# GNN kernel on one core: the adjacency build without PSUM clears, every product issued twice

## The reference, cut to what matters

```python
def _L0_gnn_ref(h, edge_src, edge_dst):
    ...
    for i in range(3):
        msg = tmp[edge_src]
        agg = jax.ops.segment_sum(msg, edge_dst, num_segments=n)
        tmp = tmp + agg / deg[:, None]
        res = res + tmp / (1.0 + i)
    return res
...
h = jnp.maximum(_layernorm(x), 0.0);  x = x + _L0_gnn_ref(h, src, dst)
h = jnp.maximum(_layernorm(x), 0.0);  x = x + _L1_gnn_ref(...)   # scatter means, MLP
h = jnp.maximum(_layernorm(x), 0.0);  x = x + _L2_gnn_ref(...)   # attention over edges
h = jnp.maximum(_layernorm(x), 0.0);  x = x + _L3_gnn_ref(...)   # equivariant convolution
```

## Time and profile before

| | us |
|---|---|
| median of 3 runs | 2495.79 |
| lowest and highest run | 2492.46 and 2499.66 |
| span of the profiled execution | 2205.5 |
| build, first to last matmul of line 1769 | 67.1 to 338.0 |
| PE, DVE, ACT busy, share of the span | 74%, 81%, 50% |

### The profile page before, as it was taken

The page is one execution under the profiler, slowest core; times in us unless marked ns, Lnnn a source line. Parts: engine busy times, 40 slices in busy tenths (PEclk is TensorE's granted clock), DMA queues, the critical chain, the costliest instruction groups (busy, mean ns, idle before and its releaser), DMA issues.

```text
span 2205.5 us, 36859 instructions
## 1 busy us (share of the span) xinstructions
PE 1640.1 (74%) x8603; PEld 1281.5 (58%) x8603; DVE 1788.0 (81%) x5309; ACT 1113.4 (50%) x2935; POOL 865.1 (39%) x861
## 2 busy tenths in 40 slices
PE   3656667998998998735678777776657788888876
PEld 2322226887887886524567676676635555555555
DVE  8898887998998995886777877878577877777776
ACT  1766666876886983200234334243544444444443
POOL 2000000000000000077777777773037777777772
PEclk8886668999999999856788888798758878777777
DMA  6355558664765764156666566563112222222221
GB/s 215 108 150 149 155 157 270 245 247 155 268 242 194 267 249 180 34 162 163 168 163 177 163 158 186 161 184 103 48 52 54 55 56 55 55 55 54 56 55 46
DMA packets 192504, 314.88 MB, mean 143 GB/s; under 512 B 25905, under 2 KB 139448, under 8 KB 182450
## 3 DMA queue, kind: packets, MB, share of 16 engines
q1 hardware_dynamic: 163344, 248.12, 34.7%
q0 software_dynamic: 27712, 63.56, 11.3%
q10 hardware_dynamic: 1250, 0.86, 0.2%
HBM read 232.38 MB, written 80.07 MB: 142 GB/s over the span
## 4 chain that ended last, share of the span: by engine, by line
POOL 24%; DVE 13%; PE 13%; issue 12%; DMA 2%; ACT 1%; SPq 1%; DVEq 0%; POOLq 0%; ACTq 0%
POOL G L704 13%; POOL G L689 7%; POOL SCR L689 5%; PE PS L1930 2%; PE PS L2037 2%; DVE HOT_R L1187 2%; PE PS L1931 2%; PE PS L1906 2%; PE PS L1821 1%; DVE GROUPED_R L1202 1%; DVE GROUPED_R L1196 1%; DMA G<-table,src_idx 1%; ACT HB L726 1%; SPq L608 1%; DVE SCR L1362 1%
## 5 line engine op out<-in xcount | busy, mean ns | idle before, releaser
L689 POOL DMA_INDIRECT G<-table,src_idx x252 | 271.2, 1076 | 969.6 <-DMA table<-RX 889.3
L704 POOL DMA_INDIRECT G<-table,gather_idx x415 | 407.4, 982 | 249.4 <-issue 123.7
L2037 PE MATMUL PS<-SCR,OH 128*128 128x256 f32 x830 | 283.0, 506 | 107.7 <-DVE SCR L1660 104.6
L2037 PEld LDWEIGHTS PS<-SCR,OH 128*128 128x128 f32 x830 | 201.6, 252 | 160.6 <-DVE SCR L1660 121.4
L1821 PE MATMUL PS<-ALL_R 128*128 128x256 f32 (+3 forms) x2025 | 267.3, 289 | 21.7 <-DVE ALL_R L1250 9.1
L1906 PE MATMUL PS<-RX,OH 128*128 x830 | 178.4, 370 | 137.3 <-DVE SCR L1362 85.8
L1821 PEld LDWEIGHTS PS<-ALL_R 128*128 128x128 f32 (+1 forms) x2025 | 252.3, 191 | 24.6 <-DVE ALL_R L1250 9.5
L1906 PEld LDWEIGHTS PS<-RX,OH 128*128 128x128 f32 x830 | 148.3, 245 | 168.9 <-issue 163.7
L1930 PE MATMUL PS<-AT 128*128 128x128 f32 x830 | 203.9, 332 | 20.0 <-issue 11.5
L1781 PE MATMUL PS<-HOT_R,GROUPED_R 128*119 128x448 f32 x830 | 194.0, 381 | 24.7 <-DVE G L1208 23.3
L1769 PE MATMUL PS<-AT,G 128*128 128x400 bf16 x474 | 142.8, 450 | 81.1 <-ACT PS L819 51.1
(11 more groups left out here) (395 smaller groups left out, 3425.2 us busy)
## 6 DMA issues: line engine op xcount, KB each, us to landing
ALL_R<-adjacency SPq DMA_DIRECT2D x72, 1600.0 KB, 6.9
adjacency<-ALL_R SPq DMA_DIRECT2D x26, 1600.0 KB, 7.4
AT<-gathered_rows SPq DMA_DIRECT2D x103, 256.0 KB, 3.8
gathered_rows<-G SPq DMA_DIRECT2D x63, 256.0 KB, 2.3
AT<-dst_in_block SPq DMA_DIRECT2D x103, 128.0 KB, 4.0
gathered_rows<-SCR SPq DMA_DIRECT2D x40, 256.0 KB, 2.2
G<-table,gather_idx POOLq DMA_INDIRECT x415, 2.6
G<-table,src_idx POOLq DMA_INDIRECT x252
```

Of the source, the lines that this page charges most:

```text
L689: pool.indirect_dma_start(score_rows(i)[:, q], None, tables[0], bass.IndirectOffsetOnAxis(ap=src_idx[:, v:v + 1], axis=0)).then_inc(s(f"sc ...
L704: pool.indirect_dma_start(G[:, p, q, :], None, tables[i], bass.IndirectOffsetOnAxis(ap=gather_idx[:, p, q:q + 1], axis=0)).then_inc(s(f"{n ...
L2037: ins = pe.matmul(PS[:, q, 0:MSG], OH[:, p, q, :], view(SCR, M_AT + (p * VB + q) * MSG, [[1, MSG]]), start=True, stop=True)
```

## The change

ACT no longer clears PSUM. Instead each visit's product is issued twice by PE, with the same operands: once overwriting (`start=True`) and once adding (`start=False`). For a visit that opens a slot, the overwriting product goes to the slot's bank and the adding one to the next slot's bank; for a visit that continues a slot, the adding product goes to the slot's bank and the overwriting one to the next slot's. What lands in the next slot's bank is overwritten when that slot is opened. A batch can now touch one bank more, so it holds 6 visits in place of 7 (`AV`), and there are 99 batches (`AB`) in place of 85. Two tables of bank offsets are loaded for each batch, 7 words and 6 words, in place of one of 8. PE waits on `pair_copied` (with an offset of 4 that ACT adds at the start) in place of `banks_zeroed`. The tables are made by DVE (four small instructions in place of three) and POOL (`place_banks`, five instructions on one partition, put between two attribute gathers); PE and ACT wait once for them.

```diff
-AV = 7
+AV = 6
-        bank_words = begins[0:1, 2 * NT + 602:2 * NT + 602 + AB * BANK_W].bitcast(I32)
+        BANK_W = 8
+        begin_words = begins[0:1, WORDS_AT:WORDS_AT + AB * BANK_W].bitcast(I32)
+        add_words = means[0:1].rearrange("p a b -> p (a b)")[:, 0:AB * BANK_W].bitcast(I32)
...
-                sp.wait_ge(s("pair_copied"), min(PER_BLK * (b + 1) + OVER, SLOTS) // 2)
+                sp.wait_ge(s("pair_copied"), OPEN + min(PER_BLK * (b + 1) + OVER, SLOTS) // 2)
...
+            def place_banks():
+
+                pool.wait_ge(s("words_made"), 1)
+                at = lambda offset, n: view(EI, offset, [[1, n]], 1).bitcast(I32)
+                pool.memset(at(STEP_AT, 1), 1)
+                pool.tensor_tensor(at(STEP_AT + 1, AB * AV - 1), at(SLOT_AT + 1, AB * AV - 1), at(SLOT_AT, AB * AV - 1), ALU.subtract)
+                pool.tensor_tensor(span, begin_at, add_at, ALU.subtract).then_inc(s("banks_paired"), 1)
+                pool.wait_ge(s("banks_paired"), 1)
+                pool.tensor_tensor(span, span, opens, ALU.mult).then_inc(s("banks_paired"), 1)
+                pool.wait_ge(s("banks_paired"), 2)
+                pool.tensor_tensor(add_at, add_at, span, ALU.add)
+                pool.tensor_tensor(begin_at, begin_at, span, ALU.subtract).then_inc(s("banks_paired"), 1)
...
+                if g == 1:
+                    place_banks()
...
+            act.wait_ge(s("banks_paired"), 3)
             copy_fills(KINDS_AT, LAST_ATTRS)
...
-            zeros2 = view(zeros_b, 0, [[0, 2], [1, KEYS]])
-            for j in range(BANKS // 2):
-                act.copy(banks(j), zeros2).then_inc(s("banks_zeroed"), 2)
+            for j in range(OPEN):
+                act.sem_inc(s("pair_copied"))
...
                 ins.then_inc(s("pair_copied"), 1)
-                if j < (SLOTS - BANKS) // 2:
-                    act.wait_ge(s("pair_copied"), j + 1)
-                    act.copy(banks(j), zeros2).then_inc(s("banks_zeroed"), 2)
...
+            pe.wait_ge(s("banks_paired"), 3)
             for k in range(AB):
-                _, words = nc.values_load_multi_w_load_instructions(bank_words[0:1, k * BANK_W:(k + 1) * BANK_W], engines=[mybir.EngineType.PE], min_val=0, max_val=(BANKS - 1) * 512,
-                                                                    skip_runtime_bounds_check_because="a masked and shifted bank number, or the count of a slot")
-                pe.wait_ge(s("banks_zeroed"), words[AV] & 255)
+                begin_w, add_w = (nc.values_load_multi_w_load_instructions(words[0:1, k * BANK_W:k * BANK_W + n], engines=[mybir.EngineType.PE], min_val=0, max_val=(BANKS - 1) * 512,
+                                                                           skip_runtime_bounds_check_because="a masked and shifted bank number, or the count of a slot")[1]
+                                  for words, n in ((begin_words, AV + 1), (add_words, AV)))
+                pe.wait_ge(s("pair_copied"), (begin_w[AV] >> 1) & 127)
                 for q in range(min(AV, NVA - AV * k)):
                     v = AV * k + q
                     pe.wait_ge(s("visit_hot"), v + 1)
-                    pe.matmul(PSF[:, bass.ds(words[q], KEYS)], src_hot(v), key_hot(v), start=False, stop=False,
+                    pe.matmul(PSF[:, bass.ds(begin_w[q], KEYS)], src_hot(v), key_hot(v), start=True, stop=False, skip_group_check=True)
+                    pe.matmul(PSF[:, bass.ds(add_w[q], KEYS)], src_hot(v), key_hot(v), start=False, stop=False,
                               skip_group_check=True).then_inc(s("visit_built"), 1)
```

More of the change, by code:

```diff
@@ L69 @@
 BANKS = 8
-ROOM_BIT = 3 * AV
+OPEN = BANKS // 2
 HOTS = 20
@@ L87 @@
 assert GRP * NSRC >= NODES and all((s * 73 + 36) >> 11 == s * SUBW // NSRC for s in range(SUBS))
-assert NB * VB == NV and (NB - PEEL) % DEPTH == 0 and AV <= BANKS - 1 and AB * AV < GA * P and SLOTS % 2 == 0 and NVA == NT + SUBS - 1 and SPAN * P <= 4096 and SUBS % PER_BLK == 0 and OBLK == 2 and OVER < P
+assert NB * VB == NV and (NB - PEEL) % DEPTH == 0 and AV + 2 <= BANKS and AB * AV < GA * P and SLOTS % 2 == 0 and NVA == NT + SUBS - 1 and SPAN * P <= 4096 and SUBS % PER_BLK == 0 and OBLK == 2 and OVER < P
 def gnn_program(nc, x, edge_ids, last_dst, edge_attrs, species, w1a, w1b, b1, w2, row_params, wlr, wup,
@@ L246, in gnn_program, with by_visit, flat @@
         pair_words = AT[0:1, 17, 0:SLOTS // 2].bitcast(I32)
-        BANK_W = AV + 1
-        bank_words = begins[0:1, 2 * NT + 602:2 * NT + 602 + AB * BANK_W].bitcast(I32)
-        assert 2 * NT + 602 + AB * BANK_W <= 4 * NT + 600 and (HOTS - 16) * KEYS // 2 <= 2 * NT + 602 and BANK_W % 4 == 0
+        BANK_W = 8
+        WORDS_AT = 2 * NT + VW + 2
+        SLOT_AT, STEP_AT = 0, 640
+        begin_words = begins[0:1, WORDS_AT:WORDS_AT + AB * BANK_W].bitcast(I32)
+        add_words = means[0:1].rearrange("p a b -> p (a b)")[:, 0:AB * BANK_W].bitcast(I32)
+        assert WORDS_AT + AB * BANK_W <= 4 * NT + 600 and (HOTS - 16) * KEYS // 2 <= WORDS_AT and AV < BANK_W
+        assert AB * BANK_W <= NBLK * 32 and SLOT_AT + AB * AV <= STEP_AT and 2 * (NVA + 1) + AB * AV <= DEPTH * VB * P
+        def by_visit(t, offset):
+            return view(t, offset, [[BANK_W, AB], [1, AV]], 1).bitcast(I32)
+        def flat(t, offset):
+            return view(t, offset, [[AV, AB], [1, AV]], 1).bitcast(I32)
+        begin_at, add_at = by_visit(begins, WORDS_AT), by_visit(means, 0)
+        opens, span = flat(EI, STEP_AT), flat(OH, 2 * (NVA + 1))
         WIDE = (RING * PER_BLK + OVER) * SUBW
@@ L276, in src_hot @@
             return view(G, v % HOTS * P // 2, [[1, P // 2]]).bitcast(BF16)
-        def banks(pair):
-            return view(PS, pair % (BANKS // 2) * 1024, [[512, 2], [1, KEYS]])
         STEPS = []
@@ L1061, in _ @@
             dve.wait_ge(s("merge_turned"), 1)
-            subs, some = HB[0:1, 1200:1200 + AB * AV].bitcast(I32), HB[0:1, 1800:1800 + AB].bitcast(I32)
+            subs = view(EI, SLOT_AT, [[1, AB * AV]], 1).bitcast(I32)
             dve.tensor_copy(subs[:, 0:4 * P], PS[0:1, 3, 0:4 * P])
@@ L1068, in _ @@
             dve.tensor_tensor(pair_words, view(PS, 512 + P + 1, [[2, SLOTS // 2]], 1), places, ALU.add)
[L1069 to L1072, removed]
+            done(dve.tensor_scalar(add_at, flat(EI, SLOT_AT), BANKS - 1, 9, ALU.bitwise_and, ALU.logical_shift_left))
+            done(dve.tensor_scalar(begin_at, add_at, 512, None, ALU.add))
+            dve.tensor_scalar(begin_at, begin_at, (BANKS - 1) * 512, None, ALU.bitwise_and)
+            dve.tensor_scalar(view(begins, WORDS_AT + AV, [[BANK_W, AB]], 1).bitcast(I32), view(EI, SLOT_AT + AV - 1, [[AV, AB]], 1).bitcast(I32), 3, None, ALU.add).then_inc(s("words_made"), 1)
             dve.wait_ge(s("built_ids_in"), 16 * GA)
@@ L1166, in _ @@
             dve.memset(small[:, 7, :], 0.0).then_inc(s("sage_ready"), 1)
-            dve.wait_ge(s("pair_copied"), SLOTS // 2)
+            dve.wait_ge(s("pair_copied"), OPEN + SLOTS // 2)
             dve.memset(PS[:, 2, :], 0.0)
@@ L1805, in pick_means @@
                           start=True, stop=True).then_inc(s("src_means_picked"), 1)
-            pe.wait_ge(s("pair_copied"), SLOTS // 2)
+            pe.wait_ge(s("pair_copied"), OPEN + SLOTS // 2)
             pe.wait_ge(s("sage_ready"), 1)
```

## The result

| | before | changed |
|---|---|---|
| median, us (4 runs each) | 2497.72 | 2662.93 |
| lowest and highest | 2492.46, 2500.21 | 2659.21, 2670.18 |
| ratio of changed to before | | 1.0653, 95% interval 1.0618 to 1.0688 |
| build, first to last matmul | 67.1 to 338.0 | 67.4 to 501.5 |

The changed kernel is 165 us slower, and its build, counted from the start of the first matmul to the start of the last, is 163 us longer (434.1 in place of 271.0): the loss lies there. The two spans must not be compared with each other: the stages behind the build take a different time on different chips, and the profile of before seems to come from a faster one (first experiment).

The account below looks back on a forecast made before the run. DVE sets the early pace, but PE's instruction queue decides after the change: build 335 us in place of 271, +64, less 3.5 at the seam, +60.5 on 2495.8 gives 2556 us; own range 2530 to 2585, wider 2505 to 2618.

Parts of the forecast that it names:

- second load, shorter batches: Build, PE's queue: loads of 7 and 6 words take 0.55 and 0.51 us quiet, 1.61 and 1.49 during a store.
- the upper bound: Build, PE's queue: two loads at the price of eight words, a batch of 2.93 us quiet and 5.35 during a store.
- 131 / 8.0: Build: 131 us in which loads are dear because stores move data; the forecast divided it by 5.0 us a batch.
- PE's instruction queue, not its array: Build: the queue decides, 2.8 over 2.0 us a quiet batch at the upper clock, 5.0 over 4.0 during a store.
- The spacing of 0.115 us: Build, PE's queue: a register instruction and its matmul cost 0.115 us, so 1.27 us from first to last of 12.
- rival A: Build: the array decides at the lower clock, at least 4.0 us a batch, 396 us in all; 2617 us, chance 0.15.
- Rival B: Build: the second load is nearly free, 273 us in all; 2494 us, or about 2525 with half hidden; chance 0.14.
- rival C: Build: faster, only ACT's clear held PE and the queue hides its loads, some 245 us; 2466 us, chance 0.06.
- Rival D: Build: loads cost at all times what they cost during a store, 495 us; 2716 us, chance 0.03.
- The build of 430 us: Build by the skill's 200 ns a register: loads 2.6 us, batch 4.35 us; set aside for the quiet 0.59 us.
- the two ends of the stage: Ahead of the build 0; at the seam to the neighbour sums -3.5 us, ACT ending some 1.6 us behind PE.
- 290 us lie outside the instructions: Total: the profiled span of 2205.5 us has no device time of its own, so the difference joined the median, 2495.8.

Follow-up runs that it names:

- first experiment: The kernel before, unchanged, profiled again (also called experiment 1): 2199.24 us, span 2197.4 us.
- experiment 12: The changed kernel, with SP's 27 stores copying as many bytes from an input in DRAM in place of SBUF: 2557.56 us, ratio 1.0345 to the kernel before.
- experiment 9: The changed kernel with both register loads but one product a visit, bank from the first table for even visits, second for odd: 2571.28 us, ratio 1.0413.
- experiment 8: The kernel before without the clears between slots, PE waiting for the pair's copy: 2450.33 us, ratio 0.9938.
- experiments 7 and 10: The kernel before with each product issued twice, in 7 into the same place, in 10 shifted by 112 columns: ratios 1.002 and 0.9994.
- experiments 11 and 1: 11: the kernel before, ACT's clear of a pair split into two one-bank clears, 2463.22 us; 1: the kernel before, unchanged, 2199.24 us.

## Why the prediction was wrong

The forecast was slower, 2556 us, with a range to 2618; measured were 2662.9, above the range.

**The step that failed** is in "second load, shorter batches": "Between one word (0.30) and eight (0.59) a word costs 0.042, so 0.55 and 0.51 us". Two prices were joined by a straight line where the price goes in steps, as by reads of four words and of single ones. Measured were 1.05 and 0.81 us quiet and up to 3.6 and 2.7 in a store, where the prediction had 1.61 and 1.49. That lies outside both of the bounds given, since the upper bound took "two loads at the price of eight words" as the worst. With the measured durations the same sum gives 1.27 + 0.39 + 1.05 + 0.81 + 0.15 = 3.7 us a quiet batch (3.71 in the trace) and, with loads of 3.5 and 2.7, 8.0 in a store; 131 / 8.0 = 16 batches and 83 x 3.7 = 307, a build of 438 us for the 434 measured, and +164 us. The 0.15 stands for the second register operation and the hand-over between the loads (0.10 and 0.06 in the trace), which the prediction put at 0.09; over 99 batches that is 6 us. Nothing else in the sum was off by more than a few us.

**What was right.** That PE's instruction queue, not its array, would decide: the waits on issue, the table, and DVE's 167 us of waits for PE. That loads have a dear price during stores: experiment 12. The spacing of 0.115 us. That the second matmul is no cost in the array and comes with a higher clock: 0.87 in the build, where experiment 9, the same without the second products, has 0.50; so rival A, the array at the lower clock, did not come true. Its 2617 us was nearer than the forecast by chance. Rival B, a second load nearly free, is excluded by the load rows, and rival C by the same. Rival D named the right term, dear loads, for the wrong reason: they are dear by their number of reads, not at all times. The build of 430 us that the prediction works out beside it, from 0.2 us for each register, lies next to the measured 434, and that too is chance: it has 2.6 us for the two loads of every batch, where the trace has 1.87 when quiet and up to 3.6 and 2.7 in a store. That the two ends of the stage would give 0 and -3.5 us: the build starts at 67.4 and ACT's last copy trails by 1.8 us in place of 5.1.

**Also wrong:** that 290 us lie outside the instructions. The span of a run is 2 us shorter than its time in the first experiment and in the changed kernel (2657.9 and 2659.7), so the profile of before and its times most likely came from different chips. It had no effect on the sum, since only the difference in the build was added to the time.

**Where the gain of the change went.** Without clears the build can lose 17 us (experiment 8); waits for the stores' ring and for copies take the place of most of the 69 us. The changed kernel never saw even that, since its queue of 431 us was longer by far than the 271 that the build takes without it.

## What to carry to other kernels

Look at an engine's instruction queue as a resource of its own: sum its register loads, register instructions and hand-overs, and compare that with the stage. Here it cost nothing while it was below the stage's length, and set that length once it was above. A price between two measured sizes should not be drawn as a line when one of them is a round number: here the 8 words of before were two groups of four, and a batch shortened from 7 visits to 6 changed the load from 2 reads to 4. Where a table of words must be loaded, pad it to whole groups of four (75 us here), and keep such loads out of the time in which transfers read SBUF (66 us here).

## What the runs showed of the hardware

- Register loads of 1, 6, 7 and 8 words took 0.30, 0.81, 1.05 and 0.59 us on PE: by the theory of reads 1, 3, 4 and 2 reads of 0.26 to 0.30 us. While a store read SBUF a read took about 0.9 us (0.87 to 0.90 for one word on ACT, up to 1.9 for 8 words, 2.7 for 6 and 3.6 for 7). The Trainium skill, "Runtime: NRT & Kernel Launch", section "Instruction fetch mechanics", gives some 200 ns for each register, in bulk too. The page speaks of loads from HBM; for these loads from SBUF the trace does not agree: 8 registers took 0.59 us, not 1.6, and 7 took 1.05.
- A load in PE's queue doesn't stop the matmuls ahead of it, but holds back all behind it: in the changed kernel one began at 99.3 us, weight loads of matmuls ahead of it went on until 99.7, and the next came at 101.69.
- A register instruction with its matmul took 0.115 us of PE's queue. From the end of a batch's last load to its first weight load passed 0.34 us with one register operation and 0.44 with two.
- The granted clock in the build was 0.50 in experiment 9 (590 matmuls in 376 us), 0.71 before (590 in 271), 0.87 in the changed kernel (1180 in 434), 1.00 in experiment 12 (1180 in 368), and 0.96 and 0.99 in experiments 7 and 10 (1180 in 274 and 275, each over its whole build).
- The kernel before took 2201, 2466 and 2466 us on three chips, and 2498 in the runs of the result. The build has the same length in the profiles of the slower and the faster chips (270 and 272 us in experiments 11 and 1, 434 and 437 for the changed kernel), and the gathers behind the neighbour sums begin at 936 and 939 us in experiments 11 and 1; the difference lies behind that.
